# A state-space stage fused with half of two feed-forward layers: norm scaling on ScalarE, GpSimd's softplus spread over more steps, batch 1 convolved at the boundary, its gates inside the steps, and another order at the end

## What is computed

```python
def _L0_attn_ref(x, W_in, conv_w, conv_b, W_x, W_dt, b_dt, A_log, Dp, W_out):
    xz = einsum('bld,ed->ble', x, W_in)
    xp, z = split(xz, 2, axis=-1)                       # 512 channels each
    xpad = pad(xp, ((0, 0), (3, 0), (0, 0)))
    xc = silu(conv_b + sum(xpad[:, k:k + l, :] * conv_w[:, k] for k in range(4)))
    dbc = einsum('ble,fe->blf', xc, W_x)                # dt (128), B (16), C (16)
    delta = softplus(einsum('blr,er->ble', dt, W_dt) + b_dt)
    dA = exp(delta[..., None] * -exp(A_log))            # 16 states per channel
    dBx = delta[..., None] * B[:, :, None, :] * xc[..., None]
    h[t] = dA[t] * h[t - 1] + dBx[t]                    # scan over the 512 tokens
    y = (einsum('bles,bls->ble', h, C) + xc * Dp) * silu(z)
    return einsum('ble,de->bld', y, W_out)
```

## Time and profile before

| | |
|---|---|
| runs | 899.51, 901.64, 901.68 us; median 901.64 |
| the profiled execution | 899.96 us; span 897.9 |
| busy in the span | TensorE 85%, its weight loads 59%, VectorE 63%, ScalarE 46%, GpSimd 30% |
| mean granted TensorE clock | 0.953 |
| the stage with its head and tail | 78 to 424 us |
| batch 0's steps, between the batches, batch 1's steps | 114.9 to 243.4, to 279.3, to 399.5 us |

### The profile page before, as it was taken

One profiled execution on the slowest core, in us unless ns is written; L12 is line 12 of the kernel. 1 busy time (PEld: TensorE's weight loads), 2 busy tenths in 40 slices (PEclk: granted clock), 3 DMA queues, 4 the chain that ended last, 5 costly groups with the idle time before them and its releaser, 6 DMA issues.

```text
span 897.9 us, 11226 instructions
## 1 busy us (share of the span) xinstructions
PE 761.5 (85%) x4027; PEld 531.3 (59%) x4027; DVE 570.1 (63%) x973; ACT 411.5 (46%) x606; POOL 270.1 (30%) x200
## 2 busy tenths in 40 slices
PE   3998868885793788898999999997789998685997
PEld 2688544552461355557787777774457785344776
DVE  4654698998959989984556556358524546713543
ACT  3455687664238466643332333440475431263221
POOL 0002069986503878980797000001000010000000
PEclk9999989998996989999999999999999999897999
DMA  9200011221101122215101000043000241000000
GB/s 297 76 1 1 2 58 59 82 71 59 47 1 49 58 59 75 79 59 155 63 2 20 1 1 1 13 108 93 4 1 1 66 115 32 28 1 0 1 1 24
DMA packets 30669, 41.88 MB, mean 47 GB/s; under 512 B 3817, under 2 KB 20019, under 8 KB 30579
## 3 DMA queue, kind: packets, MB, share of 16 engines
q1 hardware_dynamic: 29222, 40.41, 15.1%
q10 hardware_dynamic: 1396, 0.79, 0.4%
HBM read 36.83 MB, written 4.36 MB: 46 GB/s over the span
## 4 chain that ended last, share of the span: by engine, by line
PE 51%; DVE 16%; issue 14%; ACT 8%; DMA 5%; POOL 3%; SPq 2%; DVEq 0%; ACTq 0%; POOLq 0%
PE PS L462 34%; DVE PS L1706 3%; PE PS L776 2%; DVE shared L1714 2%; PE PS L912 2%; POOL shared L2014 2%; ACT shared L1332 2%; DMA route<-scratch_c 2%; PE PS L727 2%; PE PS L810 2%; DMA scratch_k<-shared 2%; ACT shared L1281 1%; DVE route L1765 1%; SPq L1953 1%; PE PS L655 1%
## 5 line engine op out<-in xcount | busy, mean ns | idle before, releaser
L2014 POOL TENSOR_TENSOR shared<-shared,route 128x1024 f32<-128x1024 f32 x64 | 151.8, 2376 | 105.0 <-DVE shared L1714 102.7
L462 PE MATMUL PS<-xnT,weights_r 128*128 128x256 f32 (+1 forms) x744 | 162.2, 365 | 11.3 <-ACT shared L1036 7.4
L462 PE MATMUL PS<-xnT,work_r 128*128 128x512 f32 (+1 forms) x624 | 159.1, 406 | 0.0
L462 PE MATMUL PS<-weights_r,work_r 128*128 128x256 f32 (+1 forms) x1008 | 147.3, 295 | 5.5 <-POOL work_r L1980 3.7
L1714 DVE TENSOR_TENSOR_SCAN shared<-shared,PS 128x512 f32<-128x512 f32 x128 | 148.8, 1203 | 4.0 <-POOL shared L2014 3.8
L462 PEld LDWEIGHTS PS<-xnT,weights_r 128*128 128x128 f32 x744 | 120.1, 194 | 46.1 <-issue 28.6
L462 PEld LDWEIGHTS PS<-weights_r,work_r 128*128 128x128 f32 (+1 forms) x1008 | 128.1, 191 | 24.5 <-issue 15.7
L1481 DVE TENSOR_TENSOR gated<-gated,PS 128x512 f32<-128x512 f32 (+1 forms) x68 | 46.6, 686 | 136.8 <-ACT gated L1016 136.8
L462 PEld LDWEIGHTS PS<-xnT,work_r 128*128 128x128 f32 (+1 forms) x624 | 115.8, 191 | 29.2 <-issue 1.1
L776 PE MATMUL PS<-shared,cf 128*128 128x512 f32 x256 | 128.0, 625 | 1.7 <-POOL shared L2014 1.7
L1016 ACT ACTIVATE gated<-PS 128x512 f32<-128x512 f32 (+1 forms) x68 | 40.6, 597 | 177.6 <-PE PS L462 170.7
(11 more groups left out here) (188 smaller groups left out, 949.9 us busy)
## 6 DMA issues: line engine op xcount, KB each, us to landing
route<-scratch_c SPq DMA_DIRECT2D x64, 256.0 KB, 3.1
shared<-in_L_ffn_W_dram SPq DMA_DIRECT2D x3, 1024.0 KB, 13.1
scratch_k<-shared SPq DMA_DIRECT2D x12, 128.0 KB
scratch_q<-shared SPq DMA_DIRECT2D x12, 128.0 KB
shared<-scratch_k SPq DMA_DIRECT2D x8, 192.0 KB
shared<-scratch_q SPq DMA_DIRECT2D x8, 192.0 KB
mamba_w<-in_L_ffn_w_dram SPq DMA_DIRECT2D x2, 704.0 KB, 5.2
beside<-in_L_ffn_w_dram SPq DMA_DIRECT2D x2, 704.0 KB, 7.9
```

The source lines that it names most:

```text
L462: last = nc.tensor.matmul(o, lhs[l], rhs[r], start=(start and i == 0), stop=(stop and i == 2))
L2014: nc.gpsimd.tensor_tensor(hc[:, u * 2 * T:(u + 1) * 2 * T].rearrange("p (c t) -> p c t", c=2), hst[:, (t % 2) * 2 * T:(t % 2 + 1) * 2 * T] ...
```

## The change

Six edits, all in the stage's four programs and the numbers that place their steps.

1. **Norm scaling on ScalarE.** For the two norms inside the steps VectorE no longer subtracts the mean and multiplies (`norm_scale`); it writes -mean in every `norm_statistics`, and a new `norm_root` only takes the reciprocal. ScalarE's new `norm_scale` does two passes over the four 128x256 rows. The fixed steps become: statistics 24 and 1, ScalarE's root and scaling 27 and 4, `norm_root` 26 and 4, transposes 27 and 6, copy 30 and 9, low part 29 and 8.
2. **GpSimd's softplus** of chunks 2 and 3 stands in steps 2, 4, 6, 8 and 10 to 13 in place of 0 to 7; ScalarE's `logarithm` and `rounded` go to steps 2 and 8. In batch 0 unit 2's silu is asked in step 1, and its product on GpSimd is in step 1.
3. **Batch 1 is convolved at the boundary.** Chunks 2 and 3 of its xc lie where delta 0 and 1 lay and its delta 0 and 1 where xc 2 and 3 lay (`xc_of`, `delta_of`), so nothing of it waits for the outputs of batch 0. Inputs 0 and 1 are issued in steps 30 and 31. Outputs 2 and 3 of batch 0 move in among batch 1's delta products, `residual` behind its softplus and `norm_statistics(0)` into step 1.
4. **Batch 1's gates** go into the steps: products in steps 0 to 3 (the last waits for gate 0, since both use bank 7), silus in ScalarE's step 4 behind the scaling, with one more table load. In batch 0 the dt projections go between the gate products and ScalarE's gates between its silus.
5. **Side pieces of batch 1** start at step 10 instead of 6 and come three in two steps instead of five in four; both end after 32 pieces. `side_residual` comes one step after its last piece instead of two.
6. **The end.** TensorE does output 0, both last states, output 1, piece 32, outputs 2 and 3, then pieces 33 to 43; before, pieces stood between all of these. The `rest_*` semaphores are merged with `prep_*`.

```diff
+SOFTPLUS_AT = (2, 4, 6, 8, 10, 11, 12, 13)
 MAMBA_OUT = (2, 3)
-XP_BANKS, Z_BANKS, DELTA_BANKS = ((4, 5, 0, 2), (7, 1, 6, 0)), ((3, 4, 5, 0), (4, 5, 2, 3)), (0, 3, 4, 5)
-DT_BANK, BC_BANK = (3, 4), 2
+XP_BANKS, Z_BANKS, DELTA_BANKS = ((4, 5, 0, 2), (7, 1, 6, 0)), ((3, 4, 5, 0), (7, 1, 6, 7)), ((0, 3, 4, 5), (0, 1, 4, 5))
+DT_BANK, BC_BANK = (6, 7), (2, 6)
 SIDE_GATE, SIDE_LIN, SIDE_OUT = 7, 1, 6
...
-SIDE_START = 6
+SIDE_START = 10
...
-    return range(min(5 * max(t - SIDE_START, 0) // 4, LOOPED), min(5 * max(t + 1 - SIDE_START, 0) // 4, LOOPED))
+    return range(min(3 * max(t - SIDE_START, 0) // 2, LOOPED), min(3 * max(t + 1 - SIDE_START, 0) // 2, LOOPED))
...
+        homes = [[t[:, c * T:(c + 1) * T] for c in range(EC)] for t in (xc, delta)]
+        xc_of = (homes[0], homes[0][0:2] + homes[1][0:2])
+        delta_of = (homes[1], homes[0][2:4] + homes[1][2:4])
+
+        dtT, bc_rest = hc[:, 4 * T:5 * T], hst[:, 0:T]
...
+            def mamba_last_outputs(self, b):
+
+                for c in (2, 3):
+                    self.pe.wait_ge(S[MAMBA]["yf"], b * 2 + c - 1)
+                    last = self.mamba_output(c)
+                last.then_inc(down_done, 1)
...
+                    if b == 0:
+                        if c:
+                            pe.wait_ge(s["tap"], tap_at(b, c - 1, 0))
+                        self.mamba_gate(0, c)
+                        if c:
+                            step_input(c - 1)
+                    elif c:
+                        step_input(c - 1)
+                step_input(EC - 1).then_inc(s["dt"], 1)
+                if b == 0:
+                    pe.wait_ge(s["zs"], EC)
                 pe.wait_ge(s["dtT"], b + 1)
...
+                        if b:
+                            self.mamba_last_outputs(0)
...
-                    if t == (28, 3)[b]:
+                    if b == 1 and t < EC:
+                        if t == EC - 1:
+                            pe.wait_ge(s["zs"], EC + 1)
+                        self.mamba_gate(1, t)
+                    if t == (27, 6)[b]:
+                        pe.wait_ge(s["zs"], (b + 1) * EC)
                         for ch in range(DC):
                             self.norm_transpose(it + 2, ch, at=(SIDE_GATE, SIDE_LIN)[ch])
-                    if b == 0 and t == STEPS - 1:
-                        self.mamba_input(1, 0)
-
-                def output(c):
-
-                    for tc in range(TC):
-                        last = nc.tensor.matmul(bank(MAMBA_OUT[tc // 2])[:, (tc % 2) * D:(tc % 2 + 1) * D],
-                                                zs[:, c * T + tc * P:c * T + (tc + 1) * P],
-                                                WoutT[:, c * D:(c + 1) * D], start=False,
-                                                stop=(c == EC - 1 and tc % 2 == 1))
-                    return last
-
-                def filler(c, pieces):
-
-                    if b == 0 and c:
-                        self.mamba_input(1, c)
-                    if b == 1:
-                        for n in pieces:
-                            self.side_piece(1, n)
-
-                filler(1, ())
+                    if b == 0 and t >= STEPS - 2:
+                        self.mamba_input(1, t - STEPS + 2)
...
+                if b == 0:
+                    self.mamba_input(1, 2)
                 pe.wait_ge(s["scan"], HEAD + 2 * (base + STEPS))
                 for j in range(2):
                     nc.tensor.matmul(bank(MAMBA_OUT[j]), ident_b[:, :], zero_b[:, :], start=True, stop=False)
                 pe.wait_ge(s["yf0"], b + 1)
-                output(0)
-                add_state(STEPS - 2)
-                filler(0, (32, 33))
-                add_state(STEPS - 1)
-                output(1)
-                filler(2, (34, 35))
-                filler(3, (36, 37))
-                for c in (2, 3):
-                    pe.wait_ge(s["yf"], b * 2 + c - 1)
-                    last = output(c)
-                last.then_inc(down_done, 1)
-                if b == 1:
-                    for n in range(38, PIECES - 4):
-                        self.side_piece(1, n)
+                if b == 0:
+                    add_state(STEPS - 2)
+                    self.mamba_input(1, 3)
+                    add_state(STEPS - 1)
+                    self.mamba_output(0)
+                    self.mamba_output(1)
+                else:
+                    self.mamba_output(0)
+                    add_state(STEPS - 2)
+                    add_state(STEPS - 1)
+                    self.mamba_output(1)
+                    pieces(LOOPED, LOOPED + 1)
+                    self.mamba_last_outputs(1)
+                    pieces(LOOPED + 1, PIECES - 4)
                     for ch in range(DC):
                         self.norm_transpose(it + 3, ch, at=4 + ch)
-                    for n in range(PIECES - 4, PIECES - 2):
-                        self.side_piece(1, n)
+                    pieces(PIECES - 4, PIECES - 2)
...
+            def norm_scale(self, k, b):
+
+                act = self.act
+                act.wait_ge(xnT_tr, 2 * (k - 1))
+                for tc in range(TC):
+                    last = nc.scalar.activation(xn_tok[:, tc * D:(tc + 1) * D],
+                                                x_tok[:, (b * TC + tc) * D:(b * TC + tc + 1) * D], ACT.Identity,
+                                                bias=stats[:, 48 + tc:49 + tc])
+                last.then_inc(centred, 1)
+                act.wait_ge(centred, k - 3)
+                act.wait_ge(rstd_ready, k - 3)
+                for tc in range(TC):
+                    x_ = xn_tok[:, tc * D:(tc + 1) * D]
+                    last = nc.scalar.activation(x_, x_, ACT.Copy, scale=stats[:, 40 + tc:41 + tc])
+                last.then_inc(xn_done, 1)
...
-                    act.wait_ge(*((s["yf0"], 1) if c < 2 else (s["yf"], 2)))
-                nc.scalar.activation(xc[:, c * T:(c + 1) * T], bank(XP_BANKS[b][c]), ACT.Identity,
...
                         if step_of(b, up_end(i)) + 5 == t:
                             self.side_high(b, i)
-                        if step_of(b, up_end(i)) + 3 == t:
+                        if (1 if b == 0 and i == 2 else step_of(b, up_end(i)) + 3) == t:
                             if b == 1 and i == 0:
-                                act.wait_ge(s["dx_p"], 4)
+                                act.wait_ge(s["sp"], 4 * 3 - 1)
                             silu(i)
-                    if t == (28, 1)[b]:
-                        self.norm_sd(it + 2)
+                    if t in (2, 8):
+                        logarithm(2 + t // 8)
+                        rounded(2 + t // 8)
+                    if t == (27, 4)[b]:
+                        nc.scalar.preload_act_table(ACT.Sqrt)
+                        self.norm_sd(it + 2, loaded=True)
+                        self.norm_scale(it + 2, 1 - b)
+                        if b:
+                            nc.scalar.preload_act_table(ACT.Silu)
+                            for c in range(EC):
+                                gate(c)
                         nc.scalar.preload_act_table_set("natural_log_exp_and_others")
-                    if t == (31, 6)[b]:
+                    if t == (30, 9)[b]:
...
+            def norm_root(self, k):
+
+                self.dve.wait_ge(sd_ready, k)
+                nc.vector.reciprocal(stats[:, 40:44], stats[:, 36:40]).then_inc(rstd_ready, 1)
...
-                        if step_of(b, down_end(4 * h + 3)) + 2 == t:
+                        if step_of(b, down_end(4 * h + 3)) + 1 == t:
                             self.side_residual(b, h)
-                    if b == 0 and t == 25:
-                        self.norm_statistics(1)
-                    if t == (27, 2)[b]:
-                        self.norm_scale(1 - b, it + 2)
-                    if t == (30, 5)[b]:
+                    if t == (24, 1)[b]:
...
                 if b == 0:
-                    self.taps(1, (0, 1))
-                else:
-                    self.side_residual(1, 0)
+                    self.taps(1, range(EC))
+                for h in range(2):
+                    if STEPS <= step_of(b, down_end(4 * h + 3)) + 1 and down_end(4 * h + 3) < LOOPED:
...
-                        if step_of(b, up_end(i)) + 1 == t:
+                        if max(step_of(b, up_end(i)) + 1, 1 - b) == t and t < STEPS - 1:
```

155 lines of the change are left out of this document (82 added, 73 removed).

## The result

The changed kernel takes 897.60 us (median of 14 runs), the kernel before 902.27 in runs beside it; the ratio is 0.9946 with an interval of 0.9927 to 0.9965, so 4.9 us (3.2 to 6.6) faster. One of the runs beside it took 1868.34, for a reason that nothing here shows; without it their median is 902.10.

A forecast was written before the change was run, and what follows sets the result against it. VectorE bounds the steps, a chain over three engines the time between batches. Terms -2.1 - 4.0 - 7.6 + 5.4 + 0 + 0.5 = -7.8 gave 893.8 us against 901.64, range 885.5 to 898.0.

The forecast's parts named there:

- (a): Batch 0's steps: waits for GpSimd's product and the B broadcast go; scan 18 comes 3.8 us earlier, not 5.
- (b): Batch 0, step 24: the earlier residual waits 6 us instead of 3.04; of the 3.8 gained, 0.6 is kept.
- (c): Batch 0's steps: norm scaling, 3.44 us on VectorE, goes to ScalarE, which has 3 us to spare; -3.4.
- Batch 1's steps, +5.4: Batch 1's steps: 13.1 us of new work and waits takes the place of 7.7 gone.
- (d): Batch 1's steps: statistics in step 1 and the reciprocal add 2.3 us.
- (e): Batch 1, step 5: VectorE waits 4.4 us for exponential 5, behind reciprocal, scaling passes, gates; between 3.0 and 5.5.
- (f): Batch 1, step 8: `norm_low` waits 3.5 us for ScalarE's copy behind `rounded(3)`, which waits for GpSimd's third softplus piece.
- (g): Batch 1: waits for `lin` move to steps 17 and 18 and stay about as long, 1.5 and 1.4 us.
- No new waits in batch 1: Rival, batch 1's steps: (e) and (f) are covered, 7.9 us less, 885.9; chance 0.14.
- GpSimd's spread gives nothing: Rival, batch 0's steps 11 to 16: GpSimd's work holds VectorE up as long as before; 897.6 us; chance 0.12.
- The slower table loads: Rival, ScalarE: a drain makes each table load cost 1.4 us more; 896.6 us; chance 0.02.
- the slower case, TensorE's clock: Rival, batch 1: TensorE stays at 1.2 GHz after idling, 3.0 us lost per step; 905.8 with four; chance 0.07.

The follow-up runs named there:

- experiment 6: Changed kernel with GpSimd's softplus of batch 0 back in steps 0 to 7, batch 1 keeping the spread; ratio to the kernel before 0.9999.
- experiment 1: Changed kernel with batch 0's `side_residual` back at two steps after its last piece and the statistics in step 25; ratio to the kernel before 0.9886.
- experiment 2: Changed kernel with GpSimd's last `side_low` of batch 0 ahead of its step's product; ratio to the kernel before 0.9838.
- experiment 11: Changed kernel with experiments 1, 2, 3, 4 and 7 together, plus GpSimd's two zs products of batch 1 in steps 25 and 29; 879.76 us, ratio 0.9729.
- experiment 8: Changed kernel with the scaling of both norms inside the steps back on VectorE, ScalarE keeping only the root; ratio to the kernel before 0.9939.
- experiment 3: Changed kernel with ScalarE's step 4 of batch 1 reordered: gates 0 to 2 between the centring and multiplying passes; ratio to the kernel before 0.9880.
- experiment 4: Changed kernel with ScalarE's copy of batch 1's transposes in step 8 ahead of `rounded(3)`, not step 9; ratio to the kernel before 0.9885.
- experiment 5: Changed kernel with GpSimd's softplus of batch 1 back in steps 0 to 7, batch 0 keeping the spread; ratio to the kernel before 0.9876.
- experiment 7: Changed kernel with ScalarE's `side_silu` of units 0 and 1 of batch 1 one step earlier; ratio to the kernel before 0.9889.
- experiment 12: Kernel before the change with only the moves of experiments 2 and 7; ratio to the unaltered kernel before 0.9932.
- experiment 9: Changed kernel with TensorE's old order at the end, pieces between the last states and outputs; ratio to the kernel before 0.9946.

## Why the prediction was right, and where it was off

**Start of the stage, -2.1: right,** -2.27. A caution: with the same code the head takes 37.5 to 37.8 in nine of the traces of changed kernels and 36.1 to 36.2 in three; in the stretch from 80 to 88 us the granted clock was 0.79 to 0.81 in the nine and 1.00 in the three. Both profiles of the table are of the first kind (0.80 and 0.79).

**Batch 0's steps, -4.0: right in mechanism and sum,** -4.00. That the sum fits to the last digit is luck: in five other traces with the same code up to there these steps take 120.2 to 121.8 in place of 120.84, which would make the term -4.6 to -3.0; only step 24 differs much, with TensorE's clock. (a) Scan 18 came 4.2 earlier against its first scan, I said 3.8; experiment 6 shows it to be the spread. 5.7 was won up to step 11 (I said 5.0) and 1.5 lost from there to step 18, mostly to the residual at step 13, which I did not see and which costs nothing only because GpSimd would hold VectorE up as long. (b) The wait at step 24 was 6.26, I said 6, and by the links named: the residual's new place, piece 46, GpSimd's `side_low`. What I did not see is that both ends can be cured: put back alone the place gives 3.0 (experiment 1), moved alone the one `side_low` that stands behind a product gives 4.4 with the clock (experiment 2), and both together leave only 0.19 beyond 3.42 at step 24 (experiment 11, with the residual's own work then at step 25). (c) The scaling: 3.4 forecast, 2.9 measured (experiment 8).

**Between the batches, -7.6: right,** -7.79; dtT 14.6 behind the last scan, the first product 28.2 behind it, forecast 14.7 and 28.4. (The forecast's stated terms, 14.7, 12.5 and 0.9, add up to 28.1, not 28.4.)

**Batch 1's steps, +5.4: too small by 3.5.** Beyond 3.42 a step the kernel before spent 10.6 us there, the changed one 19.5. By the forecast's own terms:

| term | forecast | measured | shown by |
|---|---|---|---|
| (d) statistics, reciprocal | 2.3 | 2.7 | profile |
| (e) step 5 | 4.4 | 4.93 | experiment 3 |
| (f) step 8 | 3.5 | 3.5 | experiments 4, 5 |
| (g) steps 17 and 18 | 2.9 | 4.07 | experiment 7 |
| GpSimd, steps 21 to 29 | none | 1.69 | profile |
| gone | 7.7 | 7.96 | profile |

The mechanisms of (e) and (f) are the ones named. The step that failed is (g), "stay about as long: 1.5 and 1.4": I carried the old waits for `lin` over, and at less than they were, instead of laying out the new steps. TensorE before and then now, each time at the first up piece of a unit that shares a step with the last of the unit before (pieces 3 and 4 before, 7 and 8 now):

```profile
318.83 1.27 PE L462 MATMUL PS<-xnT,weights_r 128*128 128x256 f32 x6
322.76 1.62 PE L462 MATMUL PS<-xnT,weights_r 128*128 128x256 f32 x6 [2.66 <-ACT shared L1036]
```

```profile
332.69 1.27 PE L467 MATMUL PS<-xnT,weights_r 128*128 128x256 f32 x6
336.94 1.05 PE L467 MATMUL PS<-xnT,weights_r 128*128 128x256 f32 x6 [2.98 <-ACT shared L1076]
...
338.24 3.27 PE L807 MATMUL PS<-shared,cf 128*128 128x512 f32 x4
```

The mechanism is the old one at a new place, and one step earlier for ScalarE's part cures both (experiments 7 and 12). Before, it cost VectorE 3.41 (2.10 and 1.31 at steps 11 and 12), now 4.07 (1.85 and 3.62 at steps 17 and 18, less 1.40 for `add_skip`). So of the 1.2 that I was short, 0.5 was there before and 0.7 is growth; of that, TensorE's wait gives 0.3, and where the other 0.4 comes from stays open. (In eight traces with this order it is 4.0 to 5.3; the two above 5 are those where the four states took 3.62.) The 1.69 for GpSimd I had not priced at all: from 350 to 390 us it was busy 35.1 of 40 before and held nobody up, now it is busy 36.6 and does. Putting softplus back left these waits as they were (experiment 5), so they are not the spread's; moving the two zs products took only 0.2 of them away (experiment 11), and what brought them stays open.

**Tail, 0 +-1.5:** -0.97, all of it the order (experiment 9); the residual came 3.6 earlier, I said 2.6. **Norm, +0.5:** the rows show 0.17 and 0.08 as said; whether the rest of the program is longer by more stays open. Over the twelve traces with the operation the rest is 473.1 to 479.0, median 477.1, over the two without it 473.95 and 475.79; in the profile of the changed kernel twelve products near its end took 5.49 that took 3.04 before, at a granted clock of 0.50 (from 843 to 849 us) against 1.00, in code the change does not touch.

**The rivals.** "No new waits in batch 1" fell by the rows, "GpSimd's spread gives nothing" by experiment 6. The slower table loads fell: no gap behind the loads, and experiment 3 keeps all three. The Trainium skill (ScalarE: Activation LUTs, What ACT_TABLE_LOAD costs) has a drain of some 1.4 us behind each; the trace has 0.02, and the measurement decides. Of the slower case, TensorE's clock, a part is there (the 4.93 of step 5, the 6.26 of step 24 and the 4.07 of steps 17 and 18 hold some), but the step never stayed beyond VectorE's 3.42 for that reason.

## What to carry to other kernels

When engines with strict queues share a loop, a part moved to an idle engine is worth what stands behind it there: find each wait the moved instructions will meet, and put independent work ahead of it, or the gain returns as somebody else's wait (experiments 3 and 4). A wait that carries over to a new schedule has to be laid out anew, step by step; two moves of a few instructions gave as much as the whole change (experiment 12). And compare two profiles piece by piece at marks of the program: spans of 897.9 and 897.5 held pieces that differed by up to 9 us.

## What was not expected of the hardware

TensorE's idle time was paid twice. Behind 3.83 us of waiting six matmuls took 1.65 and four of the states 2.48, where behind 1.36 they took 0.98 and 1.88; so piece 46, which started 2.9 earlier in experiment 2 (83.7 behind the first scan in place of 86.6), shortened the stretch by 4.0. How long TensorE had idled does not settle it alone: behind 2.98 us of waiting for `lin` four states took 3.27, behind 2.97 in experiment 8 they took 1.88; gate product 3 took 2.93 behind 2.71 us of waiting and 2.01 behind 3.84 (experiment 5). Nor is the level fixed by the code: with identical instructions up to there, the stretch from scan 23 to scan 24 took 12.3 to 12.5 us in some traces and 13.8 in others, and the head 36.2 or 37.7.
